# Dense stage of a graph network with a mixture of experts: the input rows added by accumulating transfers, and the first expert tile moved ahead of the last dense tile's transposes

## What is computed

```python
xn = layernorm(x)
x = x + gnn(xn, src, dst, W1, b1, gamma, beta, W2, b2) + mix(xn, Wq, Wk, Wv, proj, Wo, bo)
x = x + ffn(layernorm(x), Wr, W1, W2)

def gnn(...):      # two graph convolutions, batch norm and relu between them
    ...
    h = gcn_conv(h, W2, b2)     # h @ W2, summed over the edges, + b2
    return relu(h)
def mix(...):      # linear attention, 16 heads, then @ Wo + bo
def ffn(x, Wr, W1, W2):         # 8 experts, each row goes to its top 2
    weights, ids = top_k(x @ Wr.T, 2);  weights = softmax(weights)
    act = value * silu(gate)    # of x @ W1[e]
    out = sum over e of router_weight[e] * (act @ W2[e])
```

## Time and profile before

| what | us |
|---|---|
| median of 3 runs (1437.85 to 1440.41) | 1439.03 |
| the profiled execution, its own time | 1441.12 |
| its span | 1439.4 |
| TensorE matmuls busy in the span | 1380.5 (96%) |
| VectorE busy | 877.1 (61%) |
| ScalarE busy | 535.6 (37%) |
| GpSimd busy | 170.6 (12%) |
| share of TensorE in the chain that ended last | 70% |

### The profile page before, as it was taken

How to read it: one execution, slowest core, us unless ns; L and a number is a source line. 1 busy time by engine, 2 the same in 40 slices (tenths; PEclk the granted TensorE clock), 3 DMA queues, 4 the chain that set the end, 5 groups by cost and what they waited for, 6 DMA issues and landing times.

```text
span 1439.4 us, 19227 instructions
## 1 busy us (share of the span) xinstructions
PE 1380.5 (96%) x7434; PEld 1262.7 (88%) x7434; DVE 877.1 (61%) x1618; ACT 535.6 (37%) x643; POOL 170.6 (12%) x169
## 2 busy tenths in 40 slices
PE   6999999999999999899999999999999989999995
PEld 5788989999999999899999999999978878888884
DVE  6555668787787788645666532445466785544423
ACT  4323244544544543414222133332211235554533
POOL 0011211101101001000000000000000244322211
PEclk9999999999999999999999999999999989999998
DMA  9765422432432433938554114222185575988764
GB/s 294 237 182 126 91 50 36 100 79 36 84 92 35 86 73 56 360 117 214 132 140 109 34 48 133 83 86 69 55 221 172 155 217 167 295 230 227 199 174 73
DMA packets 108573, 193.22 MB, mean 134 GB/s; under 512 B 32289, under 2 KB 77337, under 8 KB 106764
## 3 DMA queue, kind: packets, MB, share of 16 engines
q1 hardware_dynamic: 88563, 145.83, 34.4%
q0 software_dynamic: 19920, 46.17, 16.2%
HBM read 129.38 MB, written 72.21 MB: 140 GB/s over the span
## 4 chain that ended last, share of the span: by engine, by line
PE 70%; DMA 13%; DVE 9%; ACT 4%; issue 2%; SPq 1%; POOLq 0%; ACTq 0%; DVEq 0%
PE slot L2173 22%; PE slot L2332 13%; DMA adj_d<-stage 7%; PE slot L2224 5%; PE slot L2402 5%; PE slot L2232 5%; PE lsb L2232 5%; PE slot L2126 3%; PE kvb L2366 3%; PE slot L2112 2%; PE slot L2101 2%; DVE kT L1402 1%; DMA xn_d<-dx 1%; PE slot L2210 1%; DMA mix_d<-mixn 1%
## 5 line engine op out<-in xcount | busy, mean ns | idle before, releaser
L2173 PE MATMUL slot<-big_hi,slab_h 128*128 128x418 f32 x768 | 194.4, 361 | 5.6 <-DVE mixn L1805 2.2
L2173 PE MATMUL slot<-big_lo,slab_h 128*128 128x418 f32 x768 | 189.2, 354 | 0.0
L2173 PE MATMUL slot<-big_hi,slab_l 128*128 128x418 f32 x768 | 188.4, 353 | 0.0
L2173 PEld LDWEIGHTS slot<-big_hi,slab_h 128*128 128x128 f32 x768 | 139.6, 190 | 9.5 <-DVE mixn L1805 2.5
L2173 PEld LDWEIGHTS slot<-big_hi,slab_l 128*128 128x128 f32 x768 | 145.4, 189 | 2.2
L2173 PEld LDWEIGHTS slot<-big_lo,slab_h 128*128 128x128 f32 x768 | 145.1, 189 | 2.1
L1402 DVE TENSOR_TENSOR big_lo<-slot,big_hi 128x1024 fp32r<-128x1024 f32 (+2 forms) x70 | 63.2, 928 | 101.3 <-ACT big_hi L1124 101.1
L1004 POOL DMA_DIRECT2D adj_d<-stage x80 | 67.2, 840 | 481.6 <-ACT stage L1124 346.0
L2332 PE MATMUL slot<-adj,xs_h 125*128 125x418 f32 x480 | 118.1, 354 | 0.5 <-DVE ztmp L1402 0.5
L2332 PE MATMUL slot<-adj,xs_l 125*128 125x418 f32 x480 | 117.4, 353 | 0.0
L1406 DVE TENSOR_SCALAR oh_src<-lane,src_lo 125x125 bf16<-125x125 f16 x320 | 84.3, 264 | 27.0 <-PE kvb L1986 18.7
(11 more groups left out here) (362 smaller groups left out, 2855.3 us busy)
## 6 DMA issues: line engine op xcount, KB each, us to landing
slab_raw<-slabs_dram SPq DMA_DIRECT2D x40, 512.0 KB, 4.1
adj_d<-stage POOLq DMA_DIRECT2D x81, 117.2 KB, 3.1
plain_l<-w_dram SPq DMA_DIRECT2D x16, 512.0 KB, 7.9
w_home<-w_dram SPq DMA_DIRECT2D x8, 1024.0 KB, 5.7
plain_h<-w_dram SPq DMA_DIRECT2D x14, 512.0 KB, 5.4
adj_d<-eye_dram POOLq DMA_DIRECT2D x1, 6250.0 KB, 24.1
raw<-adj_d SPq DMA_DIRECT2D x3, 1828.8 KB
dx<-x_dram SPq DMA_DIRECT2D x10, 448.0 KB
```

The lines of the kernel that those rows point to most:

```text
L2173: mm = ten.matmul(ps[:, 512 * q:512 * q + CW], w[a][:, kt, :], big[b][:, kt, CW * q:CW * q + CW], start=(kt == 0 and c == 0), stop=(kt == ...
```

## The change

1. `x_t` is gone. SP's queue loads only `xm` from `mix_d`. A new `add_x(i)` on GpSimd waits until it has landed and issues one DMA of 125 x 1024 from x into `xm` with `accum_op=ALU.add`. VectorE waits for that DMA (`x_summed`) instead of adding, and does so ahead of the bias add.
2. GpSimd's queue takes these DMAs in between: those of tiles 0 to 7 ahead of chunk 0's scatters, that of tile 8 behind them, that of tile 9 before the last two scatters of chunk 1.
3. SP waits itself for the scatters (`listed`), and the list loads of experts 0 and 1 each have their own semaphore, so that gathers 4 and 5 wait for one list only.
4. `WP 1` moves behind `FT 7`, `WP 2` ahead of tile 9's second half; `PX 0` moves from kt 3 to kt 0 of tile 7; `FT 8` moves from kt 5 to kt 3 of tile 9's right half.
5. After tile 9, `XE 0` and a first quarter of the expert tile's matmuls (`GA`) stand around `FT 9`, a second quarter (`GB`) ahead of `R 3`, the rest behind it (`GV`).

```diff
     in_front = {6: [("RT", 0), ("RK", 0)], 7: [("PX", 0), ("RW", 0), ("RX", 0), ("SL", 0)],
-                8: [("RT", 1), ("RK", 1), ("RW", 1), ("RX", 1), ("PX", 1), ("SL", 1), ("WP", 0), ("WP", 1)],
-                NT - 1: [("WH", 2), ("WH", 3), ("NA", NT - 1)]}
+                8: [("RT", 1), ("RK", 1), ("RW", 1), ("RX", 1), ("PX", 1), ("SL", 1), ("WP", 0)],
+                NT - 1: [("WH", 2), ("WH", 3), ("NA", NT - 1), ("WP", 2)]}
...
-    o += [("RT", 2), ("WP", 2), ("RK", 2), ("RW", 2), ("FT", NT - 1), ("WP", 3), ("XE", 0), ("PX", 2), ("RX", 2), ("SL", 2),
-          ("R", LAST), ("RK", LAST), ("RW", LAST), ("XE", 1), ("RX", LAST), ("GV", 0), ("PX", LAST), ("SL", LAST), ("SM", 0)]
+    o += [("RT", 2), ("RK", 2), ("XE", 0), ("RW", 2), ("FT", NT - 1), ("GA", 0), ("PX", 2), ("RX", 2), ("SL", 2), ("WP", 3), ("XE", 1),
+          ("GB", 0), ("R", LAST), ("RK", LAST), ("RW", LAST), ("RX", LAST), ("GV", 0), ("PX", LAST), ("SL", LAST), ("SM", 0)]
...
             def load_xm(i):
                 spread(xm[i % 2][:, :], mix_d[T * i:T * i + T, :], xm_landed[i % 2])
-                spread(x_t[i % 2][:, :], x[T * i:T * i + T, :], xm_landed[i % 2])
...
+            def add_x(i):
+
+                pool.wait_ge(xm_landed[i % 2], LAND * (i // 2 + 1))
+                pool.dma_start(xm[i % 2][:, :], x[T * i:T * i + T, :], accum_op=ALU.add).then_inc(x_summed[i % 2], 16)
...
             pool.wait_ge(list_cleared, 16)
-            for c in range(AHEAD):
-                list_chunk(c)
-            pool.wait_ge(listed, 32 * CHUNKS[AHEAD - 1][1])
-            pool.sem_inc(lists_free, 1)
+            for i in range(NT - 2):
+                add_x(i)
+            list_chunk(0)
+            add_x(NT - 2)
+            pool.wait_ge(spots_ready, 2)
+            list_tiles_of(CHUNKS[1][0], CHUNKS[1][1] - 1)
+            add_x(NT - 1)
+            list_tiles_of(CHUNKS[1][1] - 1, CHUNKS[1][1])
...
-                    dve.wait_ge(xm_landed[i % 2], 2 * LAND * (i // 2 + 1))
-                    link(tt(xm[i % 2][:, :], xm[i % 2][:, :], x_t[i % 2][:, :], ALU.add))
+                    dve.wait_ge(x_summed[i % 2], 16 * (i // 2 + 1))
...
                     if k == ("XE", 0):
                         expert_rows(0)
+                    elif k == ("GA", 0):
+                        expert_tile(0, 0, 2)
+                    elif k == ("GB", 0):
+                        expert_tile(0, 2, 4)
                     elif k == ("GV", 0):
-                        expert_tile(0)
+                        expert_tile(0, 4, KD)
...
-                                if q and kt == 5:
+                                if q and kt == 3:
                                     token_transposes(("FT", i - 1))
```

More of the change, by code:

```diff
@@ L198, in steps @@
             o.append(("FT", i - 1))
+        if i == 8:
+            o.append(("WP", 1))
         o += [("N", i), ("LN2", i)]
@@ L218 @@
 OTHER = INNER | {("QP", p, 0, 0) for p in range(PAIRS - 1)}
-AMID = {(6, 3): ("RT", 0), (7, 3): ("PX", 0), (8, 1): ("RT", 1), (8, 5): ("PX", 1)}
+AMID = {(6, 3): ("RT", 0), (7, 0): ("PX", 0), (8, 1): ("RT", 1), (8, 5): ("PX", 1)}
 PSUM_KINDS = {"DG", "DT", "Z", "H", "HT", "XT", "V", "K", "Q", "KK", "QP", "AT",
@@ L321 @@
 STEPS = expert_steps()
-EXPERT_KINDS = {"WP", "WH", "W2P", "XE", "GV", "SM", "TR", "OUT", "IT"}
+EXPERT_KINDS = {"WP", "WH", "W2P", "XE", "GA", "GB", "GV", "SM", "TR", "OUT", "IT"}
 EXPERT_ORDER = [k for k in ORDER if k[0] in EXPERT_KINDS] + STEPS
@@ L462, in build @@
         flat = [at(f"flat{s}", R + 74880 + 4096 * s, [T, D]) for s in range(NFL)]
-        x_t = [at(f"x_t{s}", R + 83072 + 4096 * s, [T, D]) for s in range(2)]
         l2st = at("l2st", R + 49152, [T, NT, 12])
@@ L617, in build @@
         listed = sem("listed")
-        lists_free = sem("lists_free")
+        x_summed = [sem(f"x_summed{s}") for s in range(2)]
         list_landed = [sem(f"list_landed{e}") for e in range(3)]
@@ L887, in _ @@
                 elif k == ("N", NT - 1):
-                    sp.wait_ge(lists_free, 1)
+                    sp.wait_ge(listed, 32 * CHUNKS[AHEAD - 1][1])
                     for e in range(EARLY):
@@ L909, in _ @@
             load_w2(1)
-            sp.wait_ge(lists_free, 2)
+            sp.wait_ge(listed, 32 * NT)
             for e in range(EXP):
                 if e < EARLY:
-                    load_list(e, EARLY_TILES, PER - EARLY_TILES, list_landed[2])
+                    load_list(e, EARLY_TILES, PER - EARLY_TILES, list_landed[e])
                 elif e < EXP - 1:
@@ L1039, in list_chunk, with list_tiles_of @@
                 pool.wait_ge(spots_ready, c + 1)
-                for j in range(*CHUNKS[c]):
+                list_tiles_of(*CHUNKS[c])
+            def add_x(i):
+                pool.wait_ge(xm_landed[i % 2], LAND * (i // 2 + 1))
+                pool.dma_start(xm[i % 2][:, :], x[T * i:T * i + T, :], accum_op=ALU.add).then_inc(x_summed[i % 2], 16)
+            def list_tiles_of(a, b):
+                for j in range(a, b):
                     for w in range(2):
@@ L1068, in _ @@
                 pool.wait_ge(flat_stored[s], LAND * NT // NFL)
-            pool.wait_ge(list_landed[2], 16 * (EXP + 1))
+            pool.wait_ge(list_landed[0], 32)
             gather(EARLY * EARLY_TILES)
             for n in range(TILES - 1):
+                if n == 0:
+                    pool.wait_ge(list_landed[1], 32)
+                elif n == 1:
+                    pool.wait_ge(list_landed[2], 16 * (EXP + 1 - EARLY))
                 if n + NXG - 1 < TILES:
@@ L2243, in expert_rows, with expert_tile @@
                 rows_turned(xg[n % NXG]).then_inc(expert_full, 1)
-            def expert_tile(n):
+            def expert_tile(n, first=0, last=KD):
                 e = TILE_AT[n][0]
@@ L2250, in expert_tile @@
                     ten.wait_ge(act_done, ACTED[("R", LAST)])
-                for kt in range(KD):
+                for kt in range(first, last):
                     m = SLABS_PER * e + kt // 2
@@ L2260, in expert_tile @@
                         act_turned((n - 1) % 2).then_inc(expert_full, 1)
+                if last < KD:
+                    return
                 mm.then_inc(expert_full, 1)
```

2 lines of the change are left out of this document (removed).

## The result

The changed kernel takes 1449.20 us (median of 4 runs, 1448.07 to 1452.49), the kernel before beside it 1438.44: a ratio of 1.0080 as the runs' record has it (95% interval 1.0057 to 1.0103; the two medians alone give 1.0075). So the change costs 8 to 11 us. The forecast was slower, by 5.0, with a range up to 1448.6: the direction was right, the size about half of what was measured, and the time lay above the range.

What follows compares the result with a forecast made beforehand. TensorE was taken as the bound, never stopping mid-stage and waiting only at both ends. The terms +5.2, +0.9 and -1.1 gave +5.0 us, moving the median from 1439.03 to 1444.0 us, range 1435.5 to 1448.6.

Steps and rivals of the forecast that it cites:

- the stretch behind OUT 0: From the experts' first second product on: TensorE busy to the end, gathers wait for fewer lists, no cost or gain.
- Start, tile 0: the costly place.: Tile 0's bias add must wait for its x rows, so FT 0 starts at 1065.5 instead of 1060.35: +5.2 us.
- The price of the DMA: Accumulating DMA of tile 0's x rows: 5.6 us alone, 8.9 beside loads; 8.9 taken, range ends 3.1 and 12.
- The issue: GpSimd issues tile 0's x DMA at 1050.1: xm there at 1049.6, plus an estimated 0.5 us to wake.
- The clock behind the stall: After TensorE stands 6.6 us before FT 0, half clock makes 3.4 us to the next product 4.3: +0.9 us.
- Tiles 1 to 7, nothing: Middle tiles' x rows land before their bias adds, covered by some 12 us of matmuls: no cost.
- The -0.9 before tile 9: TensorE's 0.89 us wait at tile 9's first product goes, with one slab less ahead of FT 7's low part.
- Tiles 8 and 9: The 0.9 gain is given back: x 8 late behind eight scatters, FT 8 stalls 2.0 us, nothing added to the end.
- The expert tile moved forward: Behind tile 9: TensorE gains 2.6 us, but the first silu stands behind chunk 3's exp: -1.1 us, bounds -4.8 and +2.2.
- A quick accumulate: Rival, 26%: tile 0's accumulate takes 5.6 us (1440.3 us in total) or 3.3 or less (1437.9).
- Five engines: Rival, 4%: 125 rows use 5 of 16 DMA engines, DMA takes 13.7 us, every tile late; +24, 1463 us.
- The end pays: Rival, 20%: x 0 comes early and TensorE, not the silu, sets the first second product; -3.5, 1435.5 us.

Runs made afterwards that it cites:

- tile 0 alone repaired: Changed kernel, but tile 0's x rows loaded by SP's queue and added by VectorE: 1439.55 us, ratio 0.9995 to the kernel before.
- the transfers alone: Changed kernel with the old order of names, keeping accumulating transfers, GpSimd's queue and list loads: 1446.86 us, ratio 1.0056 to the kernel before.
- holding the slabs back: Changed kernel, but two weight slabs on SP's queue wait until x of tiles 0 and 1 has landed: 1445.62 us, ratio 1.0052.
- the kernel with VectorE at both ends: Changed kernel, but x rows of tiles 0, 8 and 9 loaded and added by VectorE: 1439.95 us, ratio 1.0004.
- the two profiles: Changed kernel as it is, profiled at its first measurement (1449.20 us, ratio 1.0080) and when run once more (1447.26 us, ratio 1.0057).
- the order alone: Changed kernel without accumulating transfers, x_t loaded and added by VectorE, new order and list loads kept: 1438.40 us, ratio 0.9999.
- three repairs of a late row: Changed kernel with tile 8's x earlier (1453.95 us); also tile 9's earlier (1452.92); or also FT 8's low part before tile 9's half sum (1454.19).

## Why the prediction was right, and where it failed

The direction and the costly place were right, and the time was outside the stated range. Three terms were too small or taken as nothing: the first transfer (8.9 us, measured 10.8), tile 8's late rows ("This does not add to the end", measured XE 0 some 2.6 us later behind tile 9's first product), and the stretch behind OUT 0 ("costs and gives nothing", measured +1.5 and +1.2).

- **Which place pays: right.** "Start, tile 0: the costly place." With tile 0 alone repaired the ratio is 0.9995; with the transfers alone the loss is there in full.
- **The price of the DMA: the term that was too small.** I took 8.9 us, between ends of 3.1 and 12; it took 10.8. The split was right in kind: 5.6 alone was forecast, 5.5 measured, both in the middle tiles and at tile 0 with nothing beside it. The sharing was worth 5.3 us, not 3.3; two slabs, the bias rows and tile 1's xm were all issued on SP's queue just before, and holding the slabs back took 3.6 off. The Trainium skill ("DMA: Bandwidth & Descriptors", on queues, rings and completion order) says that each DMA engine takes turns between the queues that have work for it; 10.8 us beside SP's full queue against 5.5 alone agrees with that. The share of busy engines does not give the price by itself: with the slabs held back it was 1.00 as well, and the transfer took 7.2.
- **The issue.** Forecast 4.1 us after the common product, measured 2.9 and 3.9 in the two profiles. No row gave the 0.5 us in it for GpSimd to wake; in the changed kernel's trace 0.3 us pass from the last places of chunk 0 on VectorE (1142.99) to GpSimd's first scatter (1143.32). So x 0 was there 13.8 and 14.5 after it where 13.0 was forecast, and N 2 came 24.6 and 25.3 after it where the sum has 23.9. "+5.2, +0.9" measured +6.8 and +7.6.
- **The clock behind the stall: right.** 0.50 at FT 0, and from there to the next tile's product 4.3 us passed, as in the sum.
- **Tiles 1 to 7, nothing: right**, by the trace (no wait in N 2 to N 9) and by the kernel with VectorE at both ends. The -0.9 before tile 9 was 0.8 and 1.2.
- **Tiles 8 and 9: the step that failed in the traces.** The issue behind eight scatters came 111.8 and 112.2 us after the common product; the sum, with its own delay of 6.1 at the start, has 111.7. But the DMA took 10.3 and 10.1 us, not 8.9, FT 8 waited 2.8 and 2.6, not 2.0, and "This does not add to the end" was wrong. The gather was to be 1 to 2 us late, by the scatters, and XE 0 to stay at 1177.1. The scatters were as late as forecast, some 2 us, but with their landing, the stores of tile 8 and the list loads themselves the gather came 3.7 and 3.6 us later behind tile 9's first product than before. XE 0 had to wait for it, which the sum had ruled out, and came 2.6 later. The clock is not the cause: it fell behind FT 8's wait in the first profile (0.50 in 1173 to 1177) and not in the second (1.00), and XE 0 starts at the same place in both. With tiles 8 and 9 repaired too, XE 0 is back at 19.9.
- **The expert tile moved forward: the gain is real and is given back.** The silu chain was named as what binds, and it does: OUT 0 stands 7.2 us behind the first silu before, after, and with the order alone. From N 2 to OUT 0 the two profiles have +0.7 and +0.2, where -1.1 was forecast; with the order alone it is -0.6. Not seen: TensorE now waits 2.2 to 2.5 us before OUT 0 and works on at the lower clock, so "From there on TensorE is busy to the end" hides another +1.5 and +1.2. With the order alone it is +1.8, as much as OUT 0 had come earlier.
- **What an average execution pays of the last two stays open.** Repairing tiles 8 and 9 on top of tile 0 moved the ratio from 0.9995 to 1.0004, not down, though the trace shows XE 0 2.1 us earlier. In the profile with tile 0 alone repaired OUT 0 waited 1.88 us and the clock stayed up, in that with all three 2.17 and it fell.
- **Small misreadings.** The earlier trace rows has the bias add as tile 0's first operation; its add of x stands before it, at 1051.74. The router's operations of the earlier trace rows take 2.3 us from start to start and 2.8 to the end of the last, not 2.5. Products in steady work start 0.23 us apart, not 0.22. None of these moves the sum by more than 0.3 us.
- **The rivals.** A quick accumulate: 5.5 us where little runs beside it, but not at tile 0. Five engines: excluded, by 5.5 us in the median and by the share of 0.89 to 0.95 while tile 0's transfer moved alone, where five of 16 engines would give 0.31. The end pays: it does not, even without any accumulates (0.9999).

The sum with measured terms: +7.2 for the start, -1.0 in the middle, +2.8 behind N 9, +9.0 us, against +10.8 by the medians of the first measurement and +9.1 by those of the second (+8.2 by its ratio).

## What to carry to other kernels

Taking an operation off an engine gains only where that engine is waited for; ask first what the operation's replacement must wait for. Here it was a transfer that could start only when another had landed, at the one place where the DMA engines were full and nothing covered it; seven of ten tiles hid it, two more showed it in the traces and not in the average times, and one paid for all that the runs can tell. When a stall is moved, look at what is queued behind the new wait on its engine, and at what any other queue has behind the late step: three repairs of a late row made the kernel no faster, since they fed the next wait. A gain in one engine's order can be lost again where it then waits longer and the clock falls.
